# A tile's maximum taken one step later, ahead of the key norms; four of six tile pairs summed in plain float32; three shifts on GpSimd

## The chip, the cores and the metric

One core of one Trainium2 chip runs the whole program. It has five engines that work side by side and meet at semaphores: TensorE (PE, matrix products), VectorE (DVE), ScalarE (ACT), GpSimd (POOL), and SyncE (SP), which issues transfers. The metric is the device time of one execution in microseconds (us); lower is better.

## What is computed

A decoder layer on 16 sequences of 56 tokens, 256 channels wide: self attention, cross attention to 1500 context rows of 128 channels with 16 heads of 128, and a feed-forward block, each followed by a layer norm. The change lies in the cross attention. Cut from the reference:

```python
q = rmsnorm((hidden_states @ Wq).reshape(B, Sq, H, D), gq)
k = rmsnorm((encoder_hidden_states @ Wk).reshape(B, Skv, H, D), gk)
v = (encoder_hidden_states @ Wv).reshape(B, Skv, H, D)
scores = jnp.einsum('bqhd,bkhd->bhqk', q, k) * scale
attn = jax.nn.softmax(scores, axis=-1)
out = jnp.einsum('bhqk,bkhd->bqhd', attn, v).reshape(B, Sq, H * D) @ Wo
```

## The kernel before, in words

The kernel never forms k or v. The queries are carried into the context's space beforehand, so the scores of a tile of 125 context rows are a product of the context with them, and the values are the context itself; the value and output projections are applied behind it. What is left of k is its norm: for each context row and head, the mean square of the projected key. The kernel gets it by a product of the context with a Gram matrix of the key weights and a row-wise sum of that product times the context ("key norms").

**Batches, halves, steps.** `each_phase` runs a body for one batch after another (a phase, `ph`). A phase has 24 steps `j`; the first 12 are a half with heads 0 to 7, the others one with heads 8 to 15; `t` is the step in its half. In step j tile t (125 context rows, 12 tiles) is scored against 8 heads x 56 queries = 448 columns. Beside this the key norms of the *next* batch are made, tile j // 2, 8 heads a step. Each engine has its own body with the same steps, so the order of the instructions on an engine is written out by hand, and everything that crosses between engines waits on a counting semaphore.

**TensorE, a step** (L1518 to L1580): projection c = 0 for the norms (2 matmuls of 512 columns, L1496, L1497), scores (3 matmuls of 448, L1485 to L1487, output `xa_s_ps`), in step t = 9 the denominator (L1545, L1547), in t = 1 the turning of the maxima (L1505), in t = 2 their spreading (L1513), projection c = 1 (3 matmuls of 512, output `xa_k_ps`), then the value product (output `xa_o_ps`) of the tile scored 21 steps before (`PV_LAG`). The projections go round three banks of `k_ps`: c = 1 of step j needs the bank that c = 0 of step j - 1 filled, so it waits for the semaphore `formed` (VectorE's norms of step j - 1, L1558); c = 0 of step j waits for `squared`, ScalarE's squares of step j - 2 (L1525). The scores go round two banks of `s_ps`, freed by `s_taken`.

**VectorE, a step** (L1380 to L1463): key norms of four heads from c = 0 (L1393), scaling of the raw scores by the inverse key norm into `scores` (L1408), the running maximum over tiles (L1422, which waits for the scaling just before it); in t = 1 the maximum of the turned maxima (L1413); in some steps a shift (L1441), which subtracts the maximum from a pair of tiles of the half before; in t = 9 the closing of the half before (L1454 to L1460).

**ScalarE, a step** (L1278 to L1344): rounding of context tiles (`split_high`, L1269; `round_m`, L1276), copy of the spread maximum (L1289, t = 2), inverse of the denominator (L1294, L1296, t = 9), the exponential of the pair scored 15 steps before (L1306), for split pairs once more rounded (L1308), the rounding of value tiles (L1317), squares of the four other heads from c = 1 (L1323), and in t = 7 the rounding of the denominator (L1328).

**GpSimd, a step** (L1190 to L1248): the remainders of all that ScalarE rounds (L1155, L1175, L1199, L1239 for the probabilities, L1245 for the values), the shifts that VectorE doesn't do (L1214), the sum of the exponentials (L1225), its folding (L1232).

**Plain and split sums.** The value product of a tile is either one plain float32 matmul on `probs` (L1579) or three on rounded parts (L1574: high x high, high x low, low x high). `PAIR_SPLITS` says for the six pairs of a half how many of the two tiles are split; here the first three pairs are plain, the other three split. A split pair costs ScalarE a second exponential and GpSimd a subtraction; the value tiles that meet a split one need rounding too (`NAT_PARTS`), which is done at the steps of `NAT_HI_AT` on ScalarE and `NAT_LO_AT` on GpSimd. The rounding may not overwrite a tile that the batch before still uses, and waits for that value product (L1316).

Of the kernel before, what the change touches and what calls it, by code (L numbers as in the profile page):

```python
# [21 lines left out]
ALU = mybir.AluOpType  # L22
# [4 lines left out]
C, SK = 128, 1500  # L27
# [7 lines left out]
KT = 12  # L35
KP = SK // KT
UH = 8
UW = UH * T
# [753 lines left out]
def wait(eng, s, value):  # L792

    if not isinstance(value, int) or value > 0:
        eng.wait_ge(s, value)


STEPS = 2 * KT
# [12 lines left out]
GH = 4  # L811
QC = 4
HALF = 0.5 * XD ** -0.5
MEAN = HALF / XD
MT = 4
# [8 lines left out]
def pos_s(ph, j):  # L824

    h, t = divmod(j, KT)
    if ph.b is not None:
        u = 2 * ph.b + h
        return KT * u + t + (u - 2 + (t > TD) if u >= 2 else 0)
    return ph.at(2 * (KT + 1), (KT + 1) * h + t - 2 + (t > TD))  # L830
# [37 lines left out]
def ended_half(ph, h):  # L868

    return ph.b is None or 1 <= 2 * ph.b + h <= 2 * B  # L870
# [11 lines left out]
    return ph.at(2 * ADDS, ADDS * half + max(k, 1))  # L882


VECTOR_SHIFTS = {2: 0, 3: 2, 5: 4, 7: 6}
VS, GS = 4, 2


def vector_shifts(y):
# [11 lines left out]
    return ph.at(2 * GS, GS * (y // KT) + y % KT // 2 + 1 - VS)  # L901


FIRST_SPLIT = 3
PAIR_SPLITS = (0, 0, 0, 2, 2, 2)
SPLIT_TILES = [2 * i + o for i, n in enumerate(PAIR_SPLITS) for o in range(2 - n, 2)]
LAST_SPLITS = (0, 0, 0, 1, 1, 1)
NAT_PARTS = slice(6, 8), slice(8, 10), slice(10, 12)
LAST_PARTS = slice(7, 8), slice(9, 10), slice(11, 12)
NAT_ENDS = 8, 10, KT  # L910


def tiles_of(part):
# [14 lines left out]


NAT_PLACES = 10  # L930
NAT_HI_AT = {17: (0, 1), 21: (2,)}
NAT_LO_AT = {18: (0, 1), 23: (2,)}
SC = 20
SPLIT_PAIRS = KT // 2 - FIRST_SPLIT


def pairs_split(ph, y):

    return ph.at(2 * SPLIT_PAIRS, SPLIT_PAIRS * (y // KT) + max(y % KT // 2 + 1 - FIRST_SPLIT, 0))

# [30 lines left out]
def cross_attention(nc, a, qo, wk_parts, ctxT_in, ctxT_lo, probs, probs_r, wk_in, wk_loaded, ctxT_loaded, vo, vo_loaded,  # L971
# [6 lines left out]
    with ctx:  # L978
# [16 lines left out]
        ctx_m = sb("xa_ctx_m", [KP, KT, C])  # L995
        cmax = sb("xa_cmax", [P, UW])
# [5 lines left out]
        ss = sb("xa_ss", [KP, KT, XH])  # L1002
# [10 lines left out]
        k_ps = ctx.enter_context(nc.psum_tensor("xa_k_ps", [P, 3, 512], F32))  # L1013
        max_ps = ctx.enter_context(nc.psum_tensor("xa_max_ps", [P, 512], F32))
# [3 lines left out]
        def score_slot(ph, j):  # L1018
            return scores[0:KP, ph.at(STEPS, j) % SC, :, :].rearrange("p h q -> p (h q)")
# [25 lines left out]
        def m_count(ph, part):  # L1045
            return KT // MT * (ph.b + 1) + part + 1
# [7 lines left out]
        k_done, squared, formed = sem("xa_k_done"), sem("xa_squared"), sem("xa_formed")  # L1054
        m_loaded = [sem(f"xa_m_loaded{i}") for i in range(KT // MT)]
        m_hi_ready, m_ready = sem("xa_m_hi_ready"), sem("xa_m_ready")
# [8 lines left out]
        s_done, s_taken = sem("xa_s_done"), sem("xa_s_taken")  # L1065
        max_done, gmax_ready = sem("xa_max_done"), sem("xa_gmax_ready")
        ident_loaded, ident_ready = sem("xa_ident_loaded"), sem("xa_ident_ready")
        max_turned, qmax_ready, max_spread = sem("xa_max_turned"), sem("xa_qmax_ready"), sem("xa_max_spread")
# [308 lines left out]
        def _(dve):  # L1377
            link = linker(dve, mlp.dve_chain)

            def body(ph):  # L1380
                for j in range(STEPS):
                    h, t = divmod(j, KT)
                    if ph.b == 0 and j == 0:
                        dve.wait_ge(mlp.whi_stored, 32)
                        dve.wait_ge(mlp.wlo_stored, 32)
                    if ph.within(-1, 14):
                        if j % (2 * MT) == 0:
                            dve.wait_ge(m_ready, m_count(ph, j // (2 * MT)))
                        dve.wait_ge(k_done, ph.at(2 * STEPS, 2 * STEPS + 2 * j + 1))
                        for g in range(GH):  # L1390
                            cols = k_ps[0:KP, (2 * j) % 3, g * C:(g + 1) * C]
                            head = UH * (j % 2) + g
                            form = dve.tensor_tensor_reduce(cols, cols, ctx_m[:, j // 2, :], 2 * MEAN, 0.0, ALU.mult, ALU.add,  # L1393
                                                            ss[:, j // 2, head:head + 1])
                        form.then_inc(formed, 1)
                    if ph.within(0, 15):
                        wait(dve, s_done, pos_s(ph, j) + 1)
                        if j in (0, 6):
# [3 lines left out]
                        if t == 0:  # L1402
# [5 lines left out]
                        dve.tensor_tensor(scores[0:KP, ph.at(STEPS, j) % SC, :, :], raw, key_scale, ALU.mult  # L1408
                                          ).then_inc(s_taken, 1)

                    if t == MAX_TURN and ended_half(ph, h):
                        dve.wait_ge(max_turned, ph.at(2, h))
                        dve.tensor_reduce(qmax[:, :],  # L1413
                                          o_ps[0:QW, 1 - h, 0:QC * KP].rearrange("p (c k) -> p c k", c=QC),
                                          AX.X, ALU.max).then_inc(qmax_ready, 1)

                    if ph.within(0, 15) and t >= 1:
                        dve.wait_ge(s_taken, pos_s(ph, j) + 1)
                        wait(dve, max_done, ph.at(2 * (KT - 1), (KT - 1) * h + t - 1))
                        if t == KT - 1:  # L1420
                            wait(dve, max_turned, ph.at(2, h))
                        dve.tensor_tensor(cmax[0:KP, :] if t == KT - 1 else max_ps[0:KP, 0:UW], score_slot(ph, j),  # L1422
                                          max_ps[0:KP, 0:UW], ALU.max).then_inc(max_done, 1)
                    for step, ahead, g in ((13, 1, slice(0, 6)), (1, 0, slice(6, 12))):
                        if not ph.shift(ahead).within(0, 15):
                            continue
# [559 lines left out]
```

## Time and profile before

| | us |
|---|---|
| median of 3 runs | 1315.98 (1315.48 to 1316.28) |
| the profiled execution | 1316.16 |
| its span, first to last instruction | 1314.4 |
| TensorE busy | 1242.9 (95%) |
| VectorE busy | 1170.7 (89%) |
| GpSimd busy | 1061.6 (81%) |
| ScalarE busy | 971.3 (74%) |

The self attention and the query path fill about the first 150 us, the cross attention the rest but for the feed-forward block in the last 60. The profile's timeline has one row an instruction. A matmul's row shows its start and a modelled end that overlaps the next one, so a step of TensorE is read from start to start. The plain float32 product appears as two matmuls (x2), and the row of the c = 0 projection after it is drawn some 0.35 us early; since that is so in each of them, differences between such rows hold. VectorE's rows overlap likewise by the time its pipeline empties: what an instruction costs is the distance to the start of the next.

### The profile page before, as it was taken

Reading aid. Unit: us, or ns where it says so; the run is one execution under the profiler, and the core shown is the slowest. Engines: PE = TensorE matmul, PEld = TensorE weight load, DVE = VectorE, ACT = ScalarE, POOL = GpSimd, SP = SyncE. Lnnn points to the kernel's source line nnn. Section 1 sums busy time; section 2 is a strip of 40 time slices with the busy share of each in tenths; the row PEclk is TensorE's granted clock in tenths of the full one; section 3 lists DMA queues with packets and bytes.
Section 4 is the critical chain, followed back from the end, with each engine's and each line's share of the span. In section 5 each row is a group of like instructions: output and inputs, shape, how many; then the busy total and the mean of one; then the engine's idle time right before and its main releaser. Section 6 shows DMA issues by size and latency. Waiting matters only on the chain.

```text
span 1314.4 us, 24031 instructions
## 1 busy us (share of the span) xinstructions
PE 1242.9 (95%) x6024; PEld 958.7 (73%) x6024; DVE 1170.7 (89%) x4434; ACT 971.3 (74%) x4019; POOL 1061.6 (81%) x937
## 2 busy tenths in 40 slices
PE   8889989999999999999999999999999999999998
PEld 5767656677777777777777777777777777778787
DVE  5865679999999999999999999999999999997655
ACT  2667886888888888888888888888888888863342
POOL 5744452889898989898989898989898989997740
PEclk9999999999999999999999999999999999999999
DMA  7050240101010101010101010101010101030300
GB/s 255 34 197 1 73 168 18 54 25 48 24 48 25 48 25 48 24 48 24 48 24 48 24 48 24 48 25 48 24 48 25 48 24 48 1 112 1 135 4 28
DMA packets 34106, 66.55 MB, mean 51 GB/s; under 512 B 3056, under 2 KB 22640, under 8 KB 32176
## 3 DMA queue, kind: packets, MB, share of 16 engines
q1 hardware_dynamic: 32976, 64.66, 14.8%
q8 instruction: 48, 0.79, 0.2%
q14 instruction: 90, 0.74, 0.2%
q10 hardware_dynamic: 992, 0.36, 0.1%
HBM read 56.89 MB, written 8.13 MB: 49 GB/s over the span
## 4 chain that ended last, share of the span: by engine, by line
POOL 45%; PE 31%; issue 15%; DVE 6%; ACT 2%; DMA 1%; POOLq 0%; ACTq 0%; DVEq 0%
POOL xa_den L1225 18%; POOL probs_r L1239 8%; POOL xa_scores L1214 6%; PE om_ps L1586 3%; PE xa_o_ps L1579 3%; POOL xa_ctx_m L1175 2%; POOL xa_den L1232 2%; POOL xa_q_lo L1149 2%; POOL xa_nat_r L1245 2%; PE xq_ps L636 2%; POOL ctxT_lo L1155 2%; PE xa_k_ps L1496 1%; DVE xa_k_ps L1393 1%; PE xa_k_ps L1485 1%; PE xa_s_ps L1485 1%
## 5 line engine op out<-in xcount | busy, mean ns | idle before, releaser
L1323 ACT ACTIVATE xa_k_ps<-xa_k_ps 125x128 f32<-125x128 f32 x1536 | 399.3, 260 | 61.9 <-PE xa_k_ps L1487 59.7
L1393 DVE CUSTOM_DVE_ANT_0 xa_k_ps<-xa_k_ps,xa_ctx_m 125x128 f32<-125x128 f32 x1536 | 399.1, 323 | 16.7 <-PE xa_k_ps L1497 14.5
L1323 ACT ACTIVATION_READ_ACCUMULATOR xa_k_ps<-xa_k_ps 125x1 f32 x1536 | 283.7, 185 | 0.0
L1225 POOL TENSOR_TENSOR xa_den<-probs,xa_den 125x896 f32<-125x896 f32 x128 | 271.6, 2122 | 5.8 <-ACT probs L1306 5.8
L1408 DVE TENSOR_TENSOR xa_scores<-xa_s_ps,xa_rk 125x448 f32<-125x448 f32 x384 | 238.1, 620 | 11.1 <-PE xa_s_ps L1487 11.0
L1496 PE MATMUL xa_k_ps<-wk_parts,xa_ctxT_hi 128*125 128x512 f32 x384 | 208.1, 542 | 34.3 <-ACT xa_k_ps L1323 30.0
L1306 ACT ACTIVATE probs<-xa_scores 125x896 f32<-125x896 f32 x192 | 181.7, 946 | 71.4 <-issue 45.7
L1393 DVE DVE_READ_ACCUMULATOR2_ANT xa_ss<- 125x1 f32 x1536 | 218.7, 142 | 0.0
L1422 DVE TENSOR_TENSOR xa_max_ps<-xa_scores,xa_max_ps 125x448 f32<-125x448 f32 x320 | 200.9, 628 | 9.9
L1239 POOL TENSOR_TENSOR probs_r<-probs,xa_p_hi 125x896 fp32r<-125x896 f32 (+1 forms) x96 | 197.7, 2059 | 0.6
L1579 PE MATMUL xa_o_ps<-probs,xa_ctx_nat 125*128 125x448 f32 x396 | 181.5, 539 | 0.0
L1485 PE MATMUL xa_k_ps<-wk_parts,xa_ctxT_hi 128*125 128x512 f32 x384 | 159.7, 416 | 5.1 <-DVE xa_ss L1393 4.0
L1486 PE MATMUL xa_k_ps<-wk_parts,xa_ctxT_hi 128*125 128x512 f32 x384 | 151.4, 394 | 0.0
L1497 PE MATMUL xa_k_ps<-wk_parts,xa_ctxT_hi 128*125 128x512 f32 x384 | 151.3, 394 | 0.0
L1487 PE MATMUL xa_k_ps<-wk_parts,ctxT_lo 128*125 128x512 f32 x384 | 151.2, 394 | 0.0
L1441 DVE TENSOR_TENSOR xa_scores<-xa_scores,xa_o_ps 125x896 f32<-125x896 f32 x130 | 140.2, 1082 | 9.2 <-ACT xa_gmax L1289 8.5
L1485 PE MATMUL xa_s_ps<-xa_q_hi,xa_ctxT_hi 128*125 128x448 f32 x384 | 145.5, 379 | 0.0
L1496 PEld LDWEIGHTS xa_k_ps<-wk_parts,xa_ctxT_hi 128*125 128x125 f32 x384 | 71.0, 185 | 98.5 <-ACT xa_k_ps L1323 65.2
L1155 POOL TENSOR_TENSOR ctxT_lo<-ctxT_in,xa_ctxT_hi 128x250 fp32r<-128x250 f32 x96 | 69.9, 728 | 89.9 <-ACT xa_ctxT_hi L1269 89.8
L1487 PE MATMUL xa_s_ps<-xa_q_hi,ctxT_lo 128*125 128x448 f32 x384 | 140.6, 366 | 0.0
L1486 PE MATMUL xa_s_ps<-xa_q_lo,xa_ctxT_hi 128*125 128x448 f32 x384 | 140.4, 366 | 0.0
L1214 POOL TENSOR_TENSOR xa_scores<-xa_scores,xa_gmax 125x896 f32<-125x896 f32 x62 | 131.6, 2123 | 0.0
(193 smaller groups left out, 2615.2 us busy)
## 6 DMA issues: line engine op xcount, KB each, us to landing
xa_ctx_m<-in_ctx SPq DMA_DIRECT2D x48, 250.0 KB
xa_ctx_nat<-in_ctx SPq DMA_DIRECT2D x16, 750.0 KB
ctxT_in<-in_ctxT SPq DMA_DIRECT2D x84, 125.0 KB, 2.1
qo<-in_xo_w SPq DMA_DIRECT2D x1, 2048.0 KB, 15.8
qo<-in_xq_w SPq DMA_DIRECT2D x1, 2048.0 KB, 16.1
vo_scratch<-qo SPq DMA_DIRECT2D x2, 1024.0 KB, 4.0
w_parts_scratch<-ws_hi SPq DMA_DIRECT2D x2, 1024.0 KB, 6.2
w_parts_scratch<-ws_lo SPq DMA_DIRECT2D x2, 1024.0 KB, 7.2
```

Source lines behind the costliest of these rows:

```text
L1214: pool.tensor_tensor(score_pair(ph, y), score_pair(ph, y), gmax_pair(y), ALU.subtract).then_inc(pool_shifted, 1)
L1225: pool.tensor_tensor(den2[:, :, :], probs_pair(y), so_far, ALU.add).then_inc(den_done, 1)
L1239: pool.tensor_tensor(probs_r[0:KP, slots, :], probs[0:KP, slots, :], p_hi[:, y // 2 % (NPR // 2), first:2, :].bitcast(F32), ALU.subtract). ...
L1323: last = act.activation(cols, cols, ACT.Square, scale=MEAN ** 0.5, accum_out=ss[:, j // 2, head:head + 1])
L1393: form = dve.tensor_tensor_reduce(cols, cols, ctx_m[:, j // 2, :], 2 * MEAN, 0.0, ALU.mult, ALU.add, ss[:, j // 2, head:head + 1])
L1408: dve.tensor_tensor(scores[0:KP, ph.at(STEPS, j) % SC, :, :], raw, key_scale, ALU.mult).then_inc(s_taken, 1)
L1422: dve.tensor_tensor(cmax[0:KP, :] if t == KT - 1 else max_ps[0:KP, 0:UW], score_slot(ph, j), max_ps[0:KP, 0:UW], ALU.max).then_inc(max_don ...
L1485: pe.matmul(out, l_hi, r_hi, start=first, stop=False)
L1486: pe.matmul(out, l_hi, r_lo, start=False, stop=False)
L1487: return pe.matmul(out, l_lo, r_hi, start=False, stop=last)
L1496: pe.matmul(out, ctxT_hi[:, i, t, :], wk_hi[:, cols], start=True, stop=False)
L1579: pe.matmul(o_ps[:, hy, 0:UW], ctx_nat[:, of.parity(), ty, :], probs[0:KP, y % NPR, :], start=(ty == 0), stop=False).then_inc(pv_done, 1)
```

## The change

The instructions of VectorE in a step get a new order: scaling of tile t, maximum of tile t - 1, then key norms. The maximum of tile 11 is taken in step 0 of the next half, where the norms stay first. Pair 3 of each half (tiles 6 and 7) is summed plainly, so its second exponential and its subtraction go, and of the six rounded value tiles four are left, in two parts instead of three; they are rounded in steps 19 and 21 instead of 17 (twice) and 21. VectorE shifts three pairs of a half instead of four, in t = 2, 4, 6 instead of 2, 3, 5, 7, and GpSimd three instead of two (pair 3 too, in t = 8). The last half keeps its own list of shifts, all on VectorE. The diff, cut to its core:

```diff
-VECTOR_SHIFTS = {2: 0, 3: 2, 5: 4, 7: 6}
-VS, GS = 4, 2
+VECTOR_SHIFTS = {2: 0, 4: 2, 6: 4}
+VS, GS = 3, 3
...
-FIRST_SPLIT = 3
-PAIR_SPLITS = (0, 0, 0, 2, 2, 2)
+FIRST_SPLIT = 4
+PAIR_SPLITS = (0, 0, 0, 0, 2, 2)
...
-LAST_SPLITS = (0, 0, 0, 1, 1, 1)
-NAT_PARTS = slice(6, 8), slice(8, 10), slice(10, 12)
-LAST_PARTS = slice(7, 8), slice(9, 10), slice(11, 12)
-NAT_ENDS = 8, 10, KT
+LAST_SPLITS = (0, 0, 0, 0, 1, 1)
+NAT_PARTS = slice(8, 10), slice(10, 12)
+LAST_PARTS = slice(9, 10), slice(11, 12)
+NAT_ENDS = 10, KT
...
-NAT_HI_AT = {17: (0, 1), 21: (2,)}
-NAT_LO_AT = {18: (0, 1), 23: (2,)}
+NAT_HI_AT = {19: (0,), 21: (1,)}
+NAT_LO_AT = {20: (0,), 23: (1,)}
...
+            def take_forms(ph, j):
+
+                if j % (2 * MT) == 0:
+                    dve.wait_ge(m_ready, m_count(ph, j // (2 * MT)))
+                dve.wait_ge(k_done, ph.at(2 * STEPS, 2 * STEPS + 2 * j + 1))
...
+            def running_max(ph, j):
+
+                h, t = divmod(j, KT)
+                dve.wait_ge(s_taken, pos_s(ph, j) + 1)
+                wait(dve, max_done, ph.at(2 * (KT - 1), (KT - 1) * h + t - 1))
...
+                    if t == 0:
+                        if ended_half(ph, h):
+                            running_max(ph if h else ph.shift(-1), (j - 1) % STEPS)
+                        if ph.within(-1, 14):
+                            take_forms(ph, j)
                     if ph.within(0, 15):
                         wait(dve, s_done, pos_s(ph, j) + 1)
...
+                    if ph.within(0, 15) and t >= 2:
+                        running_max(ph, j - 1)
...
-                    if ph.within(0, 15) and t >= 1:
-                        dve.wait_ge(s_taken, pos_s(ph, j) + 1)
...
+                    if ph.within(-1, 14) and t:
+                        take_forms(ph, j)
```

## Rows read from the trace of the kernel before

**Rows 1.** Busy us (instructions) by stretch: PE, PEld, DVE, ACT, POOL; clock, DMA share, GB/s.

```profile
660.00:740.00 80.00, 76.24 (x329) 59.01 (x328) 77.99 (x314) 64.98 (x285) 74.63 (x55) 1.00 0.11 33
```

**Rows 2.** Timeline, TensorE: steps 0, 1, 12 of batch 7, step 0 of 8.

```profile
642.18 0.74 PE L1496 MATMUL xa_k_ps<-wk_parts,xa_ctxT_hi 128*125 128x512 f32 x1
644.71 0.74 PE L1496 MATMUL xa_k_ps<-wk_parts,xa_ctxT_hi 128*125 128x512 f32 x1
...
674.49 0.75 PE L1496 MATMUL xa_k_ps<-wk_parts,xa_ctxT_hi 128*125 128x512 f32 x1
...
707.93 0.75 PE L1496 MATMUL xa_k_ps<-wk_parts,xa_ctxT_hi 128*125 128x512 f32 x1
```

**Rows 3.** Timeline, TensorE: a step with a split product, to the next step's start.

```profile
688.09 0.40 PE L1496 MATMUL xa_k_ps<-wk_parts,xa_ctxT_hi 128*125 128x512 f32 x1
...
689.17 0.40 PE L1485 MATMUL xa_k_ps<-wk_parts,xa_ctxT_hi 128*125 128x512 f32 x1
...
690.49 0.40 PE L1496 MATMUL xa_k_ps<-wk_parts,xa_ctxT_hi 128*125 128x512 f32 x1
```

**Rows 4.** Chain of waits, 600 to 740 us: start, us on the chain, what.

```profile
712.06 0.43 PE xa_o_ps L1505 x4
...
715.04 0.38 PE xa_o_ps L1513 x4
```

**Rows 5.** Timeline, VectorE, batch 7: a shift and a step, then a scaling without wait.

```profile
659.56 1.08 DVE L1441 TENSOR_TENSOR xa_scores<-xa_scores,xa_o_ps 125x896 f32<-125x896 f32 x1
660.56 0.29 DVE L1393 CUSTOM_DVE_ANT_0 xa_k_ps<-xa_k_ps,xa_ctx_m 125x128 f32<-125x128 f32 x1
...
661.52 0.62 DVE L1408 TENSOR_TENSOR xa_scores<-xa_s_ps,xa_rk 125x448 f32<-125x448 f32 x1
662.17 0.63 DVE L1422 TENSOR_TENSOR xa_max_ps<-xa_scores,xa_max_ps 125x448 f32<-125x448 f32 x1
662.71 0.29 DVE L1393 CUSTOM_DVE_ANT_0 xa_k_ps<-xa_k_ps,xa_ctx_m 125x128 f32<-125x128 f32 x1
...
679.31 0.62 DVE L1408 TENSOR_TENSOR xa_scores<-xa_s_ps,xa_rk 125x448 f32<-125x448 f32 x1
679.85 0.67 DVE L1413 TENSOR_REDUCE xa_qmax<-xa_o_ps 112x4 fp32r<-112x500 f32 x1
680.43 0.62 DVE L1422 TENSOR_TENSOR xa_max_ps<-xa_scores,xa_max_ps 125x448 f32<-125x448 f32 x1
```

**Rows 6.** Timeline, VectorE: the closing of a half, first instruction to the next norms.

```profile
670.15 0.62 DVE L1454 TENSOR_TENSOR xa_s_ps<-xa_s_ps,xa_rden 128x448 f32<-128x448 f32 x1
...
672.01 0.29 DVE L1393 CUSTOM_DVE_ANT_0 xa_k_ps<-xa_k_ps,xa_ctx_m 125x128 f32<-125x128 f32 x1
```

**Rows 7.** Timeline, ScalarE, from step 17 of batch 7 to step 2 of 8.

```profile
693.15 0.42 ACT L1317 ACTIVATE xa_nat_hi<-xa_ctx_nat 125x256 fp32r<-125x256 f32 x1 [2.64 <-PE xa_o_ps L1487]
...
709.60 0.40 ACT L1269 ACTIVATE xa_ctxT_hi<-ctxT_in 128x250 fp32r<-128x250 f32 x1
...
712.95 0.95 ACT L1306 ACTIVATE probs<-xa_scores 125x896 f32<-125x896 f32 x1 [1.47 <-issue]
...
716.27 0.53 ACT L1289 ACTIVATE xa_gmax<-xa_o_ps 125x448 f32<-125x448 f32 x1
```

**Rows 8.** Timeline, TensorE: projection c = 1 that waited for the norms of 660.56.

```profile
661.71 0.49 PE L1485 MATMUL xa_k_ps<-wk_parts,xa_ctxT_hi 128*125 128x512 f32 x1
```

**Rows 9.** Timeline, TensorE and VectorE: scores and the scaling that waited for them.

```profile
1187.46 0.36 PE L1487 MATMUL xa_s_ps<-xa_q_hi,ctxT_lo 128*125 128x448 f32 x1
...
1187.86 0.62 DVE L1408 TENSOR_TENSOR xa_scores<-xa_s_ps,xa_rk 125x448 f32<-125x448 f32 x1 [1.24 <-PE xa_s_ps L1487]
```

**Rows 10.** Timeline, GpSimd, second half of batch 7; then a group by line.

```profile
699.44 1.17 POOL L1199 TENSOR_TENSOR xa_den_lo<-xa_den,xa_den_hi 125x448 fp32r<-125x448 f32 x1
...
704.55 2.13 POOL L1214 TENSOR_TENSOR xa_scores<-xa_scores,xa_gmax 125x896 f32<-125x896 f32 x1
...
L1245 POOL TENSOR_TENSOR xa_nat_r<-xa_ctx_nat,xa_nat_hi 125x256 fp32r<-125x256 f32 x45 | 33.0, 752 | 2.0 <-ACT xa_nat_hi L1317 2.0
```

More of the change, by code:

```diff
@@ L1378, in _ @@
             link = linker(dve, mlp.dve_chain)
+            def take_forms(ph, j):
+                if j % (2 * MT) == 0:
+                    dve.wait_ge(m_ready, m_count(ph, j // (2 * MT)))
+                dve.wait_ge(k_done, ph.at(2 * STEPS, 2 * STEPS + 2 * j + 1))
+                for g in range(GH):
+                    cols = k_ps[0:KP, (2 * j) % 3, g * C:(g + 1) * C]
+                    head = UH * (j % 2) + g
+                    form = dve.tensor_tensor_reduce(cols, cols, ctx_m[:, j // 2, :], 2 * MEAN, 0.0, ALU.mult, ALU.add,
+                                                    ss[:, j // 2, head:head + 1])
+                form.then_inc(formed, 1)
+            def running_max(ph, j):
+                h, t = divmod(j, KT)
+                dve.wait_ge(s_taken, pos_s(ph, j) + 1)
+                wait(dve, max_done, ph.at(2 * (KT - 1), (KT - 1) * h + t - 1))
+                if t == KT - 1:
+                    wait(dve, max_turned, ph.at(2, h))
+                dve.tensor_tensor(cmax[0:KP, :] if t == KT - 1 else max_ps[0:KP, 0:UW], score_slot(ph, j),
+                                  max_ps[0:KP, 0:UW], ALU.max).then_inc(max_done, 1)
             def body(ph):
@@ L1385, in body @@
                         dve.wait_ge(mlp.wlo_stored, 32)
[L1386 to L1395, printed above, removed]
+                    if t == 0:
[3 more added lines that the diff above has]
+                            take_forms(ph, j)
                     if ph.within(0, 15):
@@ L1415, in body @@
                                           AX.X, ALU.max).then_inc(qmax_ready, 1)
-                    if ph.within(0, 15) and t >= 1:
-                        dve.wait_ge(s_taken, pos_s(ph, j) + 1)
[L1419 to L1423, printed above, removed]
+                    if ph.within(-1, 14) and t:
+                        take_forms(ph, j)
                     for step, ahead, g in ((13, 1, slice(0, 6)), (1, 0, slice(6, 12))):
```

## The prediction

> **What bounds the kernel now.** I read the busy time by stretches first. Between 660 and 740 us, as in every stretch of the steady part, VectorE is busy 97%, TensorE 95%, GpSimd 93%, ScalarE 81% [rows 1]. No engine stands clear of the others, so the busy shares can't say what a cheaper VectorE is worth; the hand-overs decide. The chain of waits is of little use here: it runs through GpSimd because GpSimd is rarely idle. So I read the timelines of one batch, step by step.
>
> One batch takes 65.75 us, its first half (12 steps) 32.31, its second 33.44 [rows 2]. TensorE's own step is 2.53 us with a plain float32 sum and 2.40 (mostly 2.38) with a split one [rows 2, 3]. That is: key projection c=0 0.46, scores 0.61, projection c=1 0.70, then the value product, which by the difference of the steps is 0.76 plain and 0.61 split. The turn adds 0.43, the spread 0.38 [rows 4], the denominator's two matmuls about 0.42 (an estimate from the scores' 0.61 for three). A half of its own work is 6 x 2.53 + 6 x 2.38 + 1.23 = 30.7 us.
>
> VectorE's step is 2.15: norms 0.96, scaling 0.65, maximum 0.54; a shift adds 1.00, the turned maximum 0.58, closing a half 1.86 [rows 5, 6]. A half: 12 x 2.15 + 4 x 1.00 + 0.58 + 1.86 + 0.1 = 32.3, plus about 0.4 of waiting for the spread maximum. That is the measured half. **VectorE sets the pace, and it can because it may lag**: its norms of step j can start anywhere from 0.66 us (projection done) to 2.20 or 2.35 us after TensorE's step j (worked out below), and TensorE doesn't feel it. In the second half there is also a stall: ScalarE waits 2.64 us for value product 18 before it rounds the second part of the values, and only then squares [rows 7]; TensorE's step 18 is 1.9 us long for it. VectorE, late by then, catches up in it, so it costs only about 1.1.
>
> As a test of this reading I carried three recurrences through the first half of before: a step of TensorE starts after the one before it; its projection c=1 of step j+1 starts 1.25 after the norms of j start, if that is later (norms start 660.56, waiting matmul at 661.71, 0.09 longer than one that did not wait) [rows 5, 8]; scores are ready for VectorE 0.40 after their third matmul starts [rows 9], which is 1.27 after the step. They give 32.36 against the measured 32.31.
>
> **The change, part by part.**
> Maximum one step later. It no longer waits for the scaling just before it. A reduction that doesn't wait starts 0.54 after a scaling, the maximum that waits 0.65 [rows 5]. 10 steps of a half gain 0.11: -1.1 us of VectorE.
> By the Trainium skill, VectorE: DVE Perf Modes, "The DRAIN you can't avoid", a semaphore between chained VectorE instructions costs nothing extra; then this gain would be zero, VectorE's half 1.1 longer, and the forecast up to 2 us per batch worse. The two rows speak against it, and the sum goes by them.
>
> Norms behind scaling and maximum. This is the costly part. Norms of j now start only after scores of j: at 1.27 + 0.54 + 0.54 = 2.35 after the step at the earliest. TensorE wants them started by (next step + 1.07 - 1.25) = 2.20 after a split step and 2.35 after a plain one. **The room for lagging goes from some 1.6 us to nothing.** What VectorE must do beside its 2.04-us step (shift, closing) now stops TensorE, less the 0.3 to 0.5 that it idles in each undisturbed step.
>
> Plain sums. Two more tiles of a half cost TensorE 0.15 each: its half becomes 31.0. ScalarE loses a rounding exponential (0.85) per half and two of six value tiles; GpSimd loses one 2.1-us subtraction per half and a 0.75-us value subtraction per batch [rows 10]. Moving the roundings from steps 17 and 21 to 19 and 21 takes away the stall: what they wait for is done before ScalarE arrives.
>
> Shifts. VectorE does 3 instead of 4 (-1.00), GpSimd 3 instead of 2 (+2.1). So VectorE's half is 32.3 - 1.1 - 1.0 = 30.2.
> The same recurrences for the new order, steps 0 to 11, TensorE's starts: 0, 2.53, 5.49, 8.40, 10.93, 13.59, 15.97, 18.89, 21.27, 23.97, 26.92, 29.45, next half at 32.93. TensorE waits 0.13 in step 4 (shift in 2), 0.53 in step 6 (shift in 4), 0.32 in step 8 (shift in 6), 0.95 in step 11 (closing in 9). 31.0 + 1.9 = 32.9 us, with latencies crossed only four times, so good to about 0.2. Two halves are 65.85, against 65.75.
>
> **GpSimd's third shift** lies in step 8 between the low part of the denominator and the shift of pair 8. The low part can't start before ScalarE has rounded the denominator in step 7; that stands behind the exponential of pair 4, whose shift now comes a step later on VectorE. In the second half I get the rounding's end 4.4 us after step 19, about as in before, where the low part starts at 699.44 [rows 7, 10]. From there pair 8 was shifted 7.2 us later (699.44 to 704.55, and 2.1) [rows 10]; now 7.2 + 2.1 + 0.75 = 10.05. Then ScalarE exponentiates and rounds pair 8, squares, rounds the next context tiles, 2.9 after the shift's end (split at 709.60) [rows 7]. That puts GpSimd's next half at 3.7 us after its start instead of 1.7: exponential of pair 10 at 6.6 instead of 4.7 (712.95), spread maximum copied at 9.9 instead of 8.0 (716.27) [rows 7]. In before VectorE hid that by lagging; now TensorE waits in steps 1 and 3, the shift of pair 0 starts 1.6 late, and with no room it goes through to step 8. First halves become 34.5. In them neither a value part nor a context subtraction stands between the low part and the shift of pair 8, so they hand on a delay of 1.5 only, and second halves stay at 32.9.
> A batch is then 67.4: +1.65. Cover: in first halves GpSimd reaches the denominator at 24.2, its rounding is done at 24.6; if that cover is gone, each us late costs one.
>
> **The sum.** The profiled execution took 1316.16 us (span 1314.4), 0.2 above the median 1315.98. Batches 1 to 14: 14 x 1.65 = 23.1. Batch 0 before its first shift: the loop of two steps (1.08 + 1.25 + 0.70 + 1.27 = 4.30) is as long as two VectorE steps of before: 0; one shift fewer, -1. The last batch and the tail have no norms and are TensorE's: 4 to 6 more plain tiles, +0.6. 1316.16 + 23.1 - 0.4 gives 1339.
> Bounds: per batch from -1 (latency 0.1 smaller at each crossing, GpSimd's delay absorbed) to +2.3 (it also delays second halves): 1302 to 1349.
>
> **Rivals.**
> A, the cheaper VectorE is simply paid out. All four engines lose work or gain little, the 1.9-us stall goes, TensorE's half of 31.0 plus 0.9 of waiting remains: 63.8 per batch, 1316 - 27 = 1289; with part of the waits above, up to 1312. For it: 97% of VectorE. Against: it needs VectorE to lag, which the norms' new place forbids.
> The Trainium skill's Perfetto Trace Analysis, "Identifying the Most-Contended Engine", says to relieve the busiest engine first; by that rule this rival would be the forecast.
> B, the new order binds but GpSimd's delay is absorbed: 65.85 per batch, +1.4 in all: 1317. For it: the pair 10 exponential already waits 1.47 us now without harm [rows 7].
> C, GpSimd becomes the bound in both halves: its work from den_lo on is nearly gapless, and a batch of 68.4 gives 1353. Decides once den_lo starts later than 4.7 after step 7.
> D, the edit doesn't bring the 0.11 because the maximum still waits: then waits grow by up to 0.1 in the laggard steps, 1345; inside C's side.
>
> **Chances.** Forecast (slower, 1325 to 1348) 0.47; A 0.23; B 0.17, of which half lies within the 0.2% (2.6 us) that a measurement of this kernel can tell from no change; C and D together 0.13. Faster by over 0.2%: A and a little of B, 0.26. Within: 0.09. Slower: 0.65. Range 1302 to 1350.
>
> **What would show it.** Scaling to maximum 0.54 apart; norms starting 2.35 or more after the step; TensorE's c=1 projections waiting for VectorE in steps 4, 6, 8 and 11, 1.9 us a half; no wait at the value rounding; VectorE's busy share down to about 90%; den_lo to shift of pair 8 10 us; first halves longer than second ones, the reverse of now. Wrong if VectorE still lags by more than 2.4 us without TensorE waiting, or if ScalarE's exponential of pair 10 stays before 5 us: then A or B.

## The result, and the profile of the changed kernel

| | before | after |
|---|---|---|
| median, us | 1316.13 (1315.48 to 1316.71) | 1342.8 (1342.13 to 1343.33) |
| ratio, 95% interval | | 1.0202 [1.0185, 1.022] |
| span of the profiled execution | 1314.4 | 1341.1 |
| first half, second half, batch | 32.29, 33.40, 65.69 | 34.67, 32.89, 67.56 |
| TensorE, VectorE busy | 1242.9, 1170.7 | 1270.2, 1123.6 |
| GpSimd, ScalarE busy | 1061.6, 971.3 | 1052.2, 948.6 |

The change makes the kernel 2.0% slower; 1339 was forecast. Halves and batches are read, here and below, from TensorE's projections c = 0, start to start, as means over eleven batches of the steady part (2 to 12). Single steps are read from the second matmul of that projection, whose row is not drawn early. VectorE loses 47 us of busy time, and ScalarE and GpSimd lose some too, while the time grows by 27.

The same stretch as [rows 1], busy us (instructions) of PE, PEld, DVE, ACT, POOL, then clock, DMA share and GB/s, of after:

```profile
660.00:740.00 80.00, 76.78 (x320) 56.46 (x319) 71.98 (x304) 63.77 (x283) 71.22 (x56) 1.00 0.10 30
```

VectorE falls from 77.99 to 71.98 of 80 and GpSimd from 74.63 to 71.22. TensorE, at 76.24 before, is as full as it was, and the three others are emptier; nothing in this row says why the batch takes longer. The list of waits of after does (engine, what it runs, line, who released it: us in total, times, longest):

```profile
ACT probs L1306 <- issue: 131.9, 129, 2.6
DVE xa_scores L1425 <- PE xa_s_ps L1501: 97.9, 128, 1.9
PEld xa_k_ps L1499 <- DVE xa_ss L1388: 78.7, 144, 1.4
...
PEld xa_k_ps L1510 <- ACT xa_k_ps L1323: 58.0, 72, 2.0
POOL xa_den_lo L1199 <- ACT xa_den_hi L1328: 43.9, 29, 3.7
```

VectorE now waits for scores (98 us), and TensorE waits for VectorE's norms (L1388, 79 us; in before 19.1 for the same pair). ScalarE's wait ahead of the exponential goes from 45.7 to 131.9 us, the largest of the list. It is put down to "issue"; the timelines say which engine it is for. Of the 131.9 us, 87.6 (56 exponentials) end with a shift of GpSimd and 43.5 (72) with one of VectorE, counted by whose shift ended within 0.3 us of the exponential's start.

Timeline, TensorE, after: starts of batch 7, of its second half and of batch 8, as in [rows 2], and three projections c = 1 of the first half that waited for the norms, as in [rows 8].

```profile
652.97 0.74 PE L1510 MATMUL xa_k_ps<-wk_parts,xa_ctxT_hi 128*125 128x512 f32 x1
...
667.20 0.49 PE L1499 MATMUL xa_k_ps<-wk_parts,xa_ctxT_hi 128*125 128x512 f32 x1 [0.29 <-DVE xa_ss L1388]
...
677.64 0.49 PE L1499 MATMUL xa_k_ps<-wk_parts,xa_ctxT_hi 128*125 128x512 f32 x1 [0.36 <-DVE xa_ss L1388]
...
686.44 0.49 PE L1499 MATMUL xa_k_ps<-wk_parts,xa_ctxT_hi 128*125 128x512 f32 x1 [0.70 <-DVE xa_ss L1388]
...
687.63 0.75 PE L1510 MATMUL xa_k_ps<-wk_parts,xa_ctxT_hi 128*125 128x512 f32 x1
...
720.55 0.74 PE L1510 MATMUL xa_k_ps<-wk_parts,xa_ctxT_hi 128*125 128x512 f32 x1
```

The halves of this batch are 34.66 and 32.92. The waits stand in steps 4, 8 and 11; step 6, where one was forecast too, takes 2.53 us in first halves and 2.94 in second ones. The idle time in brackets understates them: by the steps' lengths, c = 1 comes 0.5, 0.6 and 1.0 us late.

Timeline, VectorE, after, as in [rows 5]: the shift at the end of step 6, then step 7 with the scaling of tile 7, the maximum of tile 6 and the norms.

```profile
674.43 1.08 DVE L1455 TENSOR_TENSOR xa_scores<-xa_scores,xa_o_ps 125x896 f32<-125x896 f32 x1
675.43 0.62 DVE L1425 TENSOR_TENSOR xa_scores<-xa_s_ps,xa_rk 125x448 f32<-125x448 f32 x1
675.96 0.62 DVE L1399 TENSOR_TENSOR xa_max_ps<-xa_scores,xa_max_ps 125x448 f32<-125x448 f32 x1
676.49 0.29 DVE L1388 CUSTOM_DVE_ANT_0 xa_k_ps<-xa_k_ps,xa_ctx_m 125x128 f32<-125x128 f32 x1
```

The maximum starts 0.53 after the scaling, where it was 0.65; the medians are 0.54 (320 pairs) in after and 0.66 (289) in before. The shift pushes the norms of step 7 to 676.49, and the projection of TensorE's step 8 that waits for them starts at 677.64, 1.15 later, the same distance as in [rows 5, 8]. In undisturbed steps (1, 2, 4, 6 and 9 of first halves) the norms start 2.34 to 2.40 us after the step; in steps 3 and 7, behind a shift, 2.86 and 2.84.

Timeline, GpSimd, after, second half of batch 7, from the low part of the denominator to the shift of pair 8 (compare [rows 10]).

```profile
711.42 1.16 POOL L1199 TENSOR_TENSOR xa_den_lo<-xa_den,xa_den_hi 125x448 fp32r<-125x448 f32 x1 [2.44 <-ACT xa_den_hi L1328]
...
713.22 2.12 POOL L1214 TENSOR_TENSOR xa_scores<-xa_scores,xa_gmax 125x896 f32<-125x896 f32 x1
715.28 0.75 POOL L1245 TENSOR_TENSOR xa_nat_r<-xa_ctx_nat,xa_nat_hi 125x256 fp32r<-125x256 f32 x1
715.99 2.10 POOL L1225 TENSOR_TENSOR xa_den<-probs,xa_den 125x896 f32<-125x896 f32 x1
718.03 1.31 POOL L1175 TENSOR_TENSOR xa_ctx_m<-xa_ctx_m,xa_m_hi 125x512 f32<-125x512 f32 x1
719.28 2.11 POOL L1214 TENSOR_TENSOR xa_scores<-xa_scores,xa_gmax 125x896 f32<-125x896 f32 x1
```

From 711.42 to the end of the second shift, taken at 721.35 where the next instruction starts, it is 9.93 us, and there is no gap in it (the row left out is a remainder of the context, L1155). Before it GpSimd waits 2.44 us for ScalarE, so more work would have had room, but not in this place. What comes of it on ScalarE (timeline, after) and on TensorE:

```profile
721.48 0.96 ACT L1306 ACTIVATE probs<-xa_scores 125x896 f32<-125x896 f32 x1 [2.54 <-issue]
722.34 0.94 ACT L1308 ACTIVATE xa_p_hi<-xa_scores 125x896 fp32r<-125x896 f32 x1
723.18 0.26 ACT L1323 ACTIVATE xa_k_ps<-xa_k_ps 125x128 f32<-125x128 f32 x1
...
727.65 0.95 ACT L1306 ACTIVATE probs<-xa_scores 125x896 f32<-125x896 f32 x1 [1.81 <-issue]
```

```profile
724.46 0.50 PE L1510 MATMUL xa_k_ps<-wk_parts,xa_ctxT_hi 128*125 128x512 f32 x1 [0.88 <-ACT xa_k_ps L1323]
```

The exponential of pair 8 waits 2.54 us and starts 0.13 after GpSimd's shift has ended: "issue" is a wait for GpSimd here. Behind it in ScalarE's queue stand the squares, and TensorE's projection c = 0 of step 1 (724.46) waits for those. **That wait was not in the prediction**, and the experiments come down to it.

There is a second, smaller way, through VectorE, as forecast. Its shift of pair 0 in batch 7 waits for the spread maximum (timeline, VectorE, after), and TensorE's step 4 is 3.06 us in first halves and 2.59 in second ones:

```profile
663.98 1.09 DVE L1455 TENSOR_TENSOR xa_scores<-xa_scores,xa_o_ps 125x896 f32<-125x896 f32 x1 [0.56 <-ACT xa_gmax L1289]
```

### The profile page after: what moved, and what is told of

It is laid out like the page before. It is cut to its first block, busy times and chain, and to the rows that moved or that the text cites. A ratio compares the mean times of both kernels' runs of the same rounds, so it can differ in the third digit from the quotient of the medians.

```text
span 1341.1 us, 23748 instructions
## 1 busy us (share of the span) xinstructions
PE 1270.2 (95%) x5962; PEld 940.9 (70%) x5962; DVE 1123.6 (84%) x4403; ACT 948.6 (71%) x3971; POOL 1052.2 (78%) x920
## 4 chain that ended last, share of the span: by engine, by line
PE 30%; DVE 15%; issue 13%; POOL 13%; ACT 8%; DVEq 0%; POOLq 0%; ACTq 0%
PE xa_o_ps L1593 6%; DVE xa_k_ps L1388 6%; POOL xa_den L1225 5%; POOL xa_scores L1214 5%; ACT xa_k_ps L1323 4%; DVE xa_max_ps L1399 3%; PE om_ps L1600 3%; PE xa_k_ps L1499 3%; DVE xa_ss L1388 2%; PE xa_s_ps L1501 2%; PE xa_s_ps L1499 2%; PE xa_s_ps L1500 2%; PE xa_k_ps L1511 2%; PE xa_k_ps L1510 2%; PE xa_k_ps L1500 2%
## 5 line engine op out<-in xcount | busy, mean ns | idle before, releaser
L1388 DVE CUSTOM_DVE_ANT_0 xa_k_ps<-xa_k_ps,xa_ctx_m 125x128 f32<-125x128 f32 x1536 | 397.6, 319 | 11.0 <-PE xa_k_ps L1511 10.8
L1306 ACT ACTIVATE probs<-xa_scores 125x896 f32<-125x896 f32 x192 | 183.4, 955 | 177.9 <-issue 131.9
L1593 PE MATMUL xa_o_ps<-probs,xa_ctx_nat 125*128 125x448 f32 x520 | 238.3, 539 | 0.0
L1510 PE MATMUL xa_k_ps<-wk_parts,xa_ctxT_hi 128*125 128x512 f32 x384 | 219.3, 571 | 19.5 <-ACT xa_k_ps L1323 16.5
L1388 DVE DVE_READ_ACCUMULATOR2_ANT xa_ss<- 125x1 f32 x1536 | 212.7, 138 | 0.0
L1499 PE MATMUL xa_k_ps<-wk_parts,xa_ctxT_hi 128*125 128x512 f32 x384 | 169.4, 441 | 30.5 <-DVE xa_ss L1388 29.3
L1399 DVE TENSOR_TENSOR xa_max_ps<-xa_scores,xa_max_ps 125x448 f32<-125x448 f32 x320 | 197.7, 618 | 0.0
L1214 POOL TENSOR_TENSOR xa_scores<-xa_scores,xa_gmax 125x896 f32<-125x896 f32 x93 | 196.4, 2112 | 0.0
L1500 PE MATMUL xa_k_ps<-wk_parts,xa_ctxT_hi 128*125 128x512 f32 x384 | 151.4, 394 | 0.0
L1511 PE MATMUL xa_k_ps<-wk_parts,xa_ctxT_hi 128*125 128x512 f32 x384 | 151.2, 394 | 0.0
L1510 PEld LDWEIGHTS xa_k_ps<-wk_parts,xa_ctxT_hi 128*125 128x125 f32 x384 | 71.0, 185 | 97.9 <-ACT xa_k_ps L1323 58.0
L1239 POOL TENSOR_TENSOR probs_r<-probs,xa_p_hi 125x896 fp32r<-125x896 f32 (+1 forms) x64 | 131.6, 2057 | 0.4
L1499 PEld LDWEIGHTS xa_k_ps<-wk_parts,xa_ctxT_hi 128*125 128x125 f32 x384 | 71.0, 185 | 84.7 <-DVE xa_ss L1388 78.7
L1155 POOL TENSOR_TENSOR ctxT_lo<-ctxT_in,xa_ctxT_hi 128x250 fp32r<-128x250 f32 x96 | 69.9, 728 | 62.2 <-ACT xa_ctxT_hi L1269 62.1
```

The source lines that it names most:

```text
L1214: pool.tensor_tensor(score_pair(ph, y), score_pair(ph, y), gmax_pair(y), ALU.subtract).then_inc(pool_shifted, 1)
L1306: act.activation(probs_pair(y), score_pair(ph, y), ACT.Exp).then_inc(exp_done, 2)
L1499: pe.matmul(out, l_hi, r_hi, start=first, stop=False)
L1500: pe.matmul(out, l_hi, r_lo, start=False, stop=False)
L1510: pe.matmul(out, ctxT_hi[:, i, t, :], wk_hi[:, cols], start=True, stop=False)
L1593: pe.matmul(o_ps[:, hy, 0:UW], ctx_nat[:, of.parity(), ty, :], probs[0:KP, y % NPR, :], start=(ty == 0), stop=False).then_inc(pv_done, 1)
```

## The experiments

The two mechanisms of the forecast are the norms' late place (which takes away VectorE's room to lag) and GpSimd's third shift. Its rival A said that the cheaper VectorE is paid out. The first four kernels take one cause away or apply one alone; "the norms first" means that `take_forms` is called ahead of the scaling in every step.

| kernel | us | ratio to before, 95% | first, second half | batch |
|---|---|---|---|---|
| after, norms first (e1) | 1325.70 | 1.0076 [1.006, 1.0093] | 33.68, 32.72 | 66.40 |
| before, new order alone (e2) | 1343.41 | 1.0212 [1.0197, 1.0227] | 32.84, 34.80 | 67.64 |
| before, sums and shifts alone (e3) | 1342.05 | 1.02 [1.0185, 1.0215] | 34.20, 33.21 | 67.41 |
| after, a subtraction later (e4) | 1334.01 | 1.0139 [1.0124, 1.0154] | 34.00, 32.89 | 66.89 |
| after, shifts 4 and 2 (e5) | 1316.49 | 1.0003 [0.9993, 1.0012] | 32.83, 32.83 | 65.66 |
| norms first, shifts 4 and 2 (e6) | 1280.21 | 0.9727 [0.9713, 0.9742] | 31.88, 31.35 | 63.24 |
| before, plain sums alone (e7) | 1296.79 | 0.9852 [0.9838, 0.9867] | 32.12, 32.11 | 64.24 |
| e1, a subtraction later (e8) | 1316.06 | 1.0001 [0.9991, 1.0011] | 33.01, 32.71 | 65.72 |
| e1, third shift earlier (e9) | 1308.84 | 0.9948 [0.9934, 0.9963] | 34.03, 31.24 | 65.26 |
| after, third shift earlier (e10) | 1317.76 | 1.0018 [1.0009, 1.0027] | 32.95, 32.87 | 65.82 |
| before, late maximum alone (e11) | 1304.32 | 0.9915 [0.9898, 0.9931] | 31.65, 33.37 | 65.02 |
| e1, squares ahead of the exponential (e12) | 1281.28 | 0.9741 [0.9724, 0.9757] | 32.20, 31.04 | 63.23 |

**e1, the norms first again.** All else stays as in after.

```diff
+                    if ph.within(-1, 14):
+                        take_forms(ph, j)
                     if ph.within(0, 15):
                         wait(dve, s_done, pos_s(ph, j) + 1)
...
-                    if ph.within(-1, 14) and t:
-                        take_forms(ph, j)
```

> The changed kernel with the key norms put back ahead of the scaling in every step; the maximum stays one step later, and the plain sums and three GpSimd shifts stay. Theory (the norms' place took VectorE's room to lag): VectorE's half is 30.2 us and may lag again, TensorE's half of 31.0 becomes the pace, the waits in steps 4, 6, 8 and 11 go; with about 1 us left at the start of first halves a batch is 63.2 to 64.5 and the time 1280 to 1300 us. Rival (GpSimd's third shift is what costs): the norms' place matters little and the time stays at 1330 or above. Rival (the maximum's new place costs): also no better than 1330.

Measured 1325.7: a miss, between the theory's range and the rivals' 1330. It gives back 17 of the 27 us. With VectorE free to lag, the third shift still costs: the absorption on which the expectation rested isn't there.

**e2, the new order alone**: before with the new VectorE body and the old constants.

> The kernel before with nothing but the new order on VectorE (scaling, maximum of the tile before, norms); sums and shifts as before. Theory: no room to lag, four shifts of VectorE per half of which each costs about 0.65 us of TensorE's time, and the stall at the value rounding (1.9 us in step 18) is no longer caught up: halves of about 33.2 and 34.7, a batch of 68, time about 1348 (1338 to 1356). Rival (the order is harmless, GpSimd's shift costs): VectorE is 2.2 us a batch cheaper and the time falls below 1316.

Measured 1343.41, as expected. The first half is 32.84, less than the 33.2 expected, and the second 34.80 for 34.7. The stall at the value rounding is as long as in before (step 18 takes 4.35 us in both); what grows is the rest of the half, in which TensorE waits for the norms.

**e3, the sums and shifts alone**: before's VectorE body with the new constants.

```diff
-VECTOR_SHIFTS = {2: 0, 3: 2, 5: 4, 7: 6}
-VS, GS = 4, 2
+VECTOR_SHIFTS = {2: 0, 4: 2, 6: 4}
+VS, GS = 3, 3
...
-PAIR_SPLITS = (0, 0, 0, 2, 2, 2)
+PAIR_SPLITS = (0, 0, 0, 0, 2, 2)
```

> The kernel before with the plain sums, the later value rounding and three GpSimd shifts, but VectorE's order and its maximum as before. Theory: VectorE's half is 31.3 with room to lag, TensorE's 31.0, the stall in step 18 is gone: a batch of 64 to 65 and 1290 to 1307 us. Rival (GpSimd's third shift costs by itself, whatever VectorE's order): at least 1.0 us per batch slower than before, 1330 or more.

Measured 1342.05: the expectation fell, and its rival, that the third shift costs by itself, holds. Waits of e3 (same columns as above):

```profile
ACT probs L1306 <- issue: 175.3, 116, 2.5
PEld xa_k_ps L1496 <- ACT xa_k_ps L1323: 101.9, 117, 2.0
...
PEld xa_k_ps L1485 <- DVE xa_ss L1393: 25.9, 56, 1.4
```

TensorE's weight loads wait 26 us for VectorE's norms in e3 (79 in after), but 102 us for ScalarE's squares.

**e4, one GpSimd subtraction later.** The subtraction of a context part (L1175, 1.3 us) that stands between the two shifts in after is moved behind the second.

```diff
-M_AT = {6: (0, 2), 14: (1, 0), 22: (1, 1)}
+M_AT = {6: (0, 2), 14: (1, 0), 23: (1, 1)}
```

> The changed kernel with one GpSimd instruction of 1.25 us (a context subtraction, L1175 of step 22) moved behind the shift of pair 8 into step 23; no work is added or removed. Theory: the path from the low part of the denominator to the shift of pair 8 in second halves goes from 10.0 to 8.8 us, the next first half starts its shift, exponential and spread maximum 1.25 earlier, first halves go from 34.7 to 33.5 to 33.9, second halves stay at 32.9: 1326 to 1332 us. Rival (first halves are long for another reason, VectorE alone): no change, 1342.

Measured 1334.01, 2 us above the range: 8.8 us of the 11 to 17 expected. The direction is right; step 0 goes from 3.67 back to 2.53, but 0.47 of these 1.14 us come back in step 2 (3.22 to 3.69), whose end waits for squares as well.

**e5, the fourth shift back on VectorE**, and **e6, the same with the norms first**.

```diff
-VECTOR_SHIFTS = {2: 0, 4: 2, 6: 4}
-VS, GS = 3, 3
+VECTOR_SHIFTS = {2: 0, 3: 2, 5: 4, 7: 6}
+VS, GS = 4, 2
```

> The changed kernel with the third shift given back to VectorE (four shifts in t = 2, 3, 5, 7 as before, two on GpSimd); order and plain sums stay as changed. It has one part of the change less than the changed kernel. Theory now (two bounds side by side: GpSimd's path through the third shift is worth 66.4 us a batch by itself, the late norms with three VectorE shifts 65.8 by themselves, both together 67.5): without the third GpSimd shift first halves lose their extra 1.8 us, the fourth VectorE shift adds some 0.3 to each half: 33.0 to 33.3 each, a batch of 66.0 to 66.6, 1320 to 1329 us, first and second halves alike. Rival (the late norms alone carry the slowdown): stays at 1340 or goes above, since VectorE has more to do.

> Late maximum and plain sums only: norms first again, four shifts on VectorE, two on GpSimd. Theory: VectorE's half is 12 x 2.04 + 4.0 + 0.58 + 1.86 + 0.1 = 31.1 with room to lag and about 0.4 of waiting, TensorE's 31.0, GpSimd has 2.1 us less per half than before on its path: a batch of 62.8 to 64.2, 1277 to 1297 us, faster than before. Rival (the maximum's new place or the plain sums cost in a way not seen yet): at or above 1316.

e5 gives 1316.49, 3.5 us under its range, with halves of 32.83: the norms' late place uses up all that the plain sums and the late maximum gain, and no more. e6 gives 1280.21, 2.7% below before. Its stretch from 660 to 740 us:

```profile
660.00:740.00 80.00, 79.48 (x345) 61.59 (x344) 78.54 (x327) 65.03 (x294) 72.66 (x57) 1.00 0.13 38
```

TensorE is busy 99% and VectorE 98%. Both are near their own sums, 31.0 and 31.1 a half; what is left stands mainly in step 9, which takes 3.68 us in first halves and 3.25 in second ones, for 2.95.

**e7, the plain sums alone** (with the later value rounding), and **e11, the late maximum alone**, each on before.

> The kernel before with the plain sums and the later value rounding only. Theory: VectorE's half stays 32.3 to 32.7 and is the pace in both halves, the stall in step 18 is gone, GpSimd is relieved: a batch of 64.7 to 65.3, 1302 to 1311 us. Rival (0.6 us more of TensorE per batch is paid in full and the stall was covered): 1316 + 8 = 1324.

> The kernel before with only the maximum one step later; norms first, split sums, shifts and value rounding as before. Theory: VectorE's half falls by 1.1 to 31.2 with its room to lag kept; first halves about 31.7; the stall at the value rounding in second halves is now paid nearly in full, 32.6 to 33.2; a batch of 64.3 to 64.9, 1296 to 1305 us. Rival (no semaphore wait costs anything on VectorE): no change, 1316.

e7 gives 1296.79, 5 us better than its range: with the stall gone both halves take 32.1, close to the 32.3 that the forecast's sum gives VectorE. e11 gives 1304.32, within its range, though its batch, 65.02, and its second half, 33.37, lie just above theirs (64.9 and 33.2). Its gain is in the first half alone (32.29 to 31.65); in the second (33.40 in before) the stall decides, as before.

**e8, e1 with e4's edit.**

> The kernel of the first experiment (norms first, late maximum, plain sums, three GpSimd shifts) with the one context subtraction of 1.25 us on GpSimd moved from step 22 behind the shift of pair 8. Theory (that kernel's 66.4 us a batch are the round trip GpSimd - ScalarE through the third shift): 0.6 to 1.2 us a batch less, 1309 to 1318 us, all of it around the start of first halves. Rival (TensorE or VectorE is its bound): no change, 1326.

Measured 1316.06, as expected: 9.6 us for the same move, also where VectorE may lag.

**e9 and e10, GpSimd's third shift one place earlier**, in step 7 behind the sum of the exponentials, ahead of the denominator's low part; e9 on e1, e10 on after.

```diff
+                    if t == 7 and ph.b != B and ended_half(ph, h):
+                        pool_shift(ph, KT * (h - 1) + 2 * VS)
```

> The kernel of the first experiment (norms first, late maximum, plain sums, three GpSimd shifts), but GpSimd does the third shift (pair 6) in step 7, before the low part of the denominator, instead of in step 8 behind it. GpSimd's work is the same; only the place differs, and it falls into the 1.5 us in which GpSimd waits for ScalarE's rounding there. Theory (what costs is the 2.1 us between the low part and the shift of pair 8, not GpSimd's amount of work): VectorE's half 30.1, TensorE's 31.0, GpSimd's batch 61.3 busy: a batch of 62.2 to 63.3, 1265 to 1281 us. Rival (GpSimd has too much to do with three shifts): 1315 or more, like the 1326 of the first experiment.

> The changed kernel with the same move of the third GpSimd shift to step 7; the norms stay behind scaling and maximum. It leaves the late norms as the only bound. Theory: both halves are what the hand recurrences gave for TensorE and VectorE alone, 32.9 each, a batch of 65.85, 1314 to 1321 us. Rival (the late norms cost little once GpSimd is out of the way): 1300 or less.

e10 gives 1317.76, and both its halves (32.95, 32.87) are the 32.9 of the recurrence: with GpSimd's delay out of the way the late norms alone cost what the forecast's part on them said. e9 misses: 1308.84 instead of 1265 to 1281. The delay is moved, not removed. A wait of e9 (columns as above):

```profile
PEld xa_s_ps L1566 <- POOL xa_den_lo L1207: 34.0, 28, 2.1
```

The low part is now the one that is late, TensorE's denominator waits for it, and step 9 of the first halves takes 5.03 us instead of 3.06.

**e12, the squares ahead of the exponential.** e1 with the third shift in its place; ScalarE takes its squares first in steps 1, 9 and 11 of a half, in which the exponential waits for a GpSimd shift.

```diff
+                    if t in (1, 9, 11):
+                        squares(ph, j)
                     y = lagged_pair(ph, j, EXP_LAG)
...
+                    if t not in (1, 9, 11):
+                        squares(ph, j)
```

> The kernel with the norms first again (late maximum, four plain sums, three GpSimd shifts: 1325.7 us, batch 66.40), in which ScalarE now takes its squares ahead of the exponential in steps 1, 9 and 11, the steps whose exponential waits for a GpSimd shift. Theory: the third shift hurts because the squares, which TensorE's first key product of the next step needs, are queued behind the waiting exponential; ahead of it they are on time, TensorE's waits in steps 2, 10 and 12 mostly go, and the batch is 64.0 to 65.0, 1292 to 1306 us. Rival: the work of GpSimd and its round trip with ScalarE and VectorE are the bound by themselves, the waits only move to the scores or the closing step, and the batch stays at 66 to 66.8, 1318 to 1330 us.

Measured 1281.28, 44 us below e1 and better than its range. GpSimd does all its three shifts, in the same places. ScalarE and TensorE of e1, around the turn into batch 7 (timeline; GpSimd's third shift starts at 637.65):

```profile
639.85 0.96 ACT L1306 ACTIVATE probs<-xa_scores 125x896 f32<-125x896 f32 x1 [1.12 <-POOL xa_scores L1214]
...
641.01 0.26 ACT L1323 ACTIVATE xa_k_ps<-xa_k_ps 125x128 f32<-125x128 f32 x1
...
645.90 0.96 ACT L1306 ACTIVATE probs<-xa_scores 125x896 f32<-125x896 f32 x1 [2.53 <-issue]
646.76 0.94 ACT L1308 ACTIVATE xa_p_hi<-xa_scores 125x896 fp32r<-125x896 f32 x1
647.60 0.26 ACT L1323 ACTIVATE xa_k_ps<-xa_k_ps 125x128 f32<-125x128 f32 x1
```

```profile
642.29 0.50 PE L1508 MATMUL xa_k_ps<-wk_parts,xa_ctxT_hi 128*125 128x512 f32 x1 [0.73 <-ACT xa_k_ps L1323]
...
643.93 0.39 PE L1499 MATMUL xa_k_ps<-wk_parts,ctxT_lo 128*125 128x512 f32 x1
...
648.88 0.50 PE L1508 MATMUL xa_k_ps<-wk_parts,xa_ctxT_hi 128*125 128x512 f32 x1 [1.27 <-ACT xa_k_ps L1323]
```

The squares of 647.60 take a projection whose third matmul starts at 643.93 on TensorE, 3.7 us before. They, like those of 641.01, stand behind an exponential that waits, and TensorE waits for them. ScalarE of e12 in such a step (t = 9), from the second instruction of the denominator's inverse on, and GpSimd's shift for it:

```profile
650.52 0.58 ACT L1307 ACTIVATE xa_rden<-xa_rden 128x448 f32<-128x448 f32 x1
651.01 0.26 ACT L1285 ACTIVATE xa_k_ps<-xa_k_ps 125x128 f32<-125x128 f32 x1
...
652.22 0.96 ACT L1319 ACTIVATE probs<-xa_scores 125x896 f32<-125x896 f32 x1
```

```profile
650.01 2.12 POOL L1214 TENSOR_TENSOR xa_scores<-xa_scores,xa_gmax 125x896 f32<-125x896 f32 x1
```

The squares fill what was a wait, and the exponential starts as soon as the shift ends. TensorE's weight loads wait for squares as in the two rows below, first of e1, then of e12.

```profile
PEld xa_k_ps L1508 <- ACT xa_k_ps L1323: 98.6, 103, 2.0
```

```profile
PEld xa_k_ps L1515 <- ACT xa_k_ps L1285: 18.3, 46, 0.9
```

Steps 0, 10 and 22 go from 4.07, 3.27 and 3.58 us to 2.53, 2.54 and 2.53, and the second half is 31.04: the 31.0 that the forecast had for TensorE's own work. The first half keeps 1.2 us more, half of it in step 3 (3.14 for 2.52): there TensorE waits for the squares of step 2, which on ScalarE follow the exponential of step 1 and what is queued behind it without a gap. So what the third shift cost (45.5 us from e6 to e1) came not from the amount of GpSimd's work, which is the same in e12, but in the main through the order of ScalarE's queue. (Against e6, e12 still has 2.1 us a half more on GpSimd and 1.0 less on VectorE; the two are within each other's intervals.)

## Why the prediction was right, and where it was not

**The number** (1339 forecast, 1342.8 measured, both mechanisms in the trace). Of the missing 4 us the first halves, 34.67 against 34.5, make 2.4; that a batch of before is 65.69 in the mean, and 65.75 only in the batch read, makes 0.8. One figure of the reading doesn't add up: VectorE's 32.3 plus 0.4 of waiting is 32.7, and not the measured half of 32.31. It doesn't enter the sum.

**Maximum, 0.11 a step: right in size.** 0.54 for 0.66 in the median. Alone it brings 11.4 us (e11), and 16.6 on top of the plain sums (e7 to e6), where no stall hides the second half's share. The Trainium skill, VectorE: DVE Perf Modes, "The DRAIN you can't avoid", found no cost of a semaphore after each of eight copies; that does not carry over to these instructions: e11 changes little else, and is 0.85% faster.

**Norms behind scaling and maximum: right, step by step.** The recurrence's steps against the second half of after, which no delay of GpSimd reaches at its start (us; step 0 is the kernel's 12):

| step | 0 | 1 | 2 | 3 | 4 | 5 | 6 | 7 | 8 | 9 | 10 | 11 | half |
|---|---|---|---|---|---|---|---|---|---|---|---|---|---|
| forecast | 2.53 | 2.96 | 2.91 | 2.53 | 2.66 | 2.38 | 2.92 | 2.38 | 2.70 | 2.95 | 2.53 | 3.48 | 32.93 |
| measured | 2.53 | 2.96 | 2.97 | 2.52 | 2.59 | 2.38 | 2.94 | 2.39 | 2.65 | 2.94 | 3.08 | 2.93 | 32.89 |
| e10, both halves | | | | | | | | | | | | | 32.95, 32.87 |

The waits are in the steps named and 1.9 us in sum. One is shared out otherwise: of the 0.95 of step 11, 0.55 appears one step earlier, as a wait for ScalarE's squares of step 9, whose exponential waits for GpSimd's third shift; in e10, without that shift in the way, steps 10 and 11 take 2.54 and 3.48, as forecast. The term, 65.85 for a batch, is e10's 65.82.

**Plain sums: right in kind, their worth too small.** No wait at the value rounding is left in after's list (40.8 us before). The stall was put at 1.1 us; in e7 the second half falls by 1.28 though TensorE has 0.3 more to do in it, and all of e7 takes 19 us off the kernel.

**GpSimd's third shift: right in time and place, wrong in why it costs.** From the low part to the end of pair 8's shift 10.05 was forecast and 9.93 measured; the exponential of pair 10 came 6.75 us into the next half (727.65 less 720.55, and less the 0.35 by which that row is drawn early) for 6.6, and the copy of the spread maximum, in batch 7, 10.1 us (663.42) for 9.9. First halves grow longer than second ones, as said. But the forecast let the delay reach TensorE through VectorE, in steps 1 and 3, "with no room it goes through", and said that VectorE hides it by lagging where it may. For the most part it reaches TensorE in step 0 (3.67 for 2.53), through the squares, and in step 2 (3.22 for 2.97); steps 1 and 3 have no wait. Of the 1.8 us by which first halves are longer these two make 1.4, and steps 3 to 11 together the other 0.4; the path through VectorE is in step 4. That the sum of 34.5 came out is in part luck: the delay had the size forecast and mostly another way. **The step that failed is "In before VectorE hid that by lagging"**: e3 and e1 let VectorE lag as in before, and the third shift costs 45 us there. A wait was followed to the engine that receives its result, and not to what is queued behind it on the engine that waits.

**The two causes don't add.** Undoing the shift alone brings 26 us (e5), the order alone 17 (e1), both 63 (e6). They stand side by side: where one is gone the other still sets the step. In the forecast's sum the late norms and what the other edits gain cancel (65.85 for 65.75), and all of the loss is the shift's. That is right as a difference, as e5 and e10 show, but it hides that each costs 36 to 45 us by itself (e6 to e5, e6 to e1).

**The rivals.** A, the relief is paid out, gave 1289 and is what happens with the norms first and either fewer GpSimd shifts or the squares ahead (1280, 1281); the argument against it, that VectorE must be able to lag, is what e5 against e6 shows (36 us). The Trainium skill's Perfetto Trace Analysis, "Identifying the Most-Contended Engine", would have one relieve the busiest engine first; here the runs go both ways. e11, which only makes VectorE cheaper, is 0.85% faster. e3, which relieves it from 97 to 92% by giving GpSimd a shift, and leaves its order alone, is 2.0% slower; so is after, from 97 to 90%, which also moves the norms. B, 1317, is what e10 and e5 measure with GpSimd's delay out. C, GpSimd as a bound in both halves, did not come: second halves stayed at 32.89. D falls with the 0.54.

**What stays open.** e12 moves the squares in three steps at once, so which of them carries how much was not told apart. The squares ahead with the norms in their late place were not tried, nor was e6 together with e12's order. That order may gain something without the third shift as well: e6's batch is 63.24, TensorE's own two halves are 62.0, so at most 1.2 of the 3.2 us a batch between e1 and e12 (an estimate from these numbers) could be of that kind.

## What to carry to other kernels

Before an operation is moved or a wait is added, list what is queued behind it on its engine and when the consumers of *those* need it: here a third 2.1-us shift on GpSimd cost 45 us while four squares stood behind the exponential that waits for it; with them ahead the kernel was as fast (1281.3) as with that shift on VectorE (1280.2). Between engines that are all nearly full, ask how far each may lag behind the others; an order that lowers an engine's work but takes its room to lag can lose more than it saves. A cause that is undone alone shows only what it costs beyond the next bound, so undo the causes together as well.

## What the runs showed that was not expected

- A VectorE maximum over 125x448 float32 that waits for the scaling just before it starts 0.66 us after it, one that doesn't 0.54 (medians of before and after); over the kernel that is 11 to 17 us (e11, e7 to e6).
- One GpSimd subtraction of 1.3 us, moved by one step, is worth 8.8 and 9.6 us (e4, e8), about 0.7 us a batch, although GpSimd is idle for 2.44 us just ahead of the stretch in which it stands: where in an engine's idle time an instruction lies counts, not how much idle time there is.
- Relieved of most of its waits TensorE is busy 98.9 to 99.5 us of each 100 from 300 to 1100 us, at a granted clock of 1.00 in all of them (e6).
